# Searching expert slots in the running sums, routing earlier, and laying the routed experts between the last groups of shared experts

## The reference, cut to what matters

```python
E, K, G, TG, I, NSH, C = 32, 6, 8, 3, 176, 2, 48
logits = x @ gate_w.T                       # 4096 x 32
# 3 of 8 groups of experts are kept, softmax, then the 6 best experts of each token
topk_w, topk_idx = top_k(probs, K); topk_w = topk_w * 16
pos = cumsum(one_hot(flat_e, E))[flat_e] - 1   # place of this token in its expert's queue
valid = pos < C                             # only the first 48 tokens of an expert count
xb = buf[:E * C].reshape(E, C, h)           # gathered: 32 experts x 48 slots x 256
g, u = split(einsum('ech,ehf->ecf', xb, w_gate_up), 2)
yb = einsum('eci,eih->ech', silu(g) * u, w_down)
out = weighted sum of yb over a token's experts
gs, us = split(x @ ws_gate_up, 2)           # the shared expert, on all 4096 tokens
out = out + silu(gs) * us @ ws_down
```

## Time and profile before

| | |
|---|---|
| median of 3 runs | 2079.32 us (2078.84 to 2084.3) |
| the profiled execution | 2079.05 us, its span 2077.1 us, mean granted TensorE clock 0.866 |
| TensorE busy | 1750.2 us, 84% of the span |
| PE weight loads busy | 1091.0 us |
| VectorE, ScalarE, GpSimd busy | 1191.6, 805.7, 254.5 us |
| the mixture of experts | from about 445 to 835 us |

### The profile page before, as it was taken

One profiled execution on the slowest core, in us unless ns is written; L12 is line 12 of the kernel. 1 busy time (PEld: TensorE's weight loads), 2 busy tenths in 40 slices (PEclk: granted clock), 3 DMA queues, 4 the chain that ended last, 5 costly groups with the idle time before them and its releaser, 6 DMA issues.

```text
span 2077.1 us, 27028 instructions
## 1 busy us (share of the span) xinstructions
PE 1750.2 (84%) x10042; PEld 1091.0 (53%) x10043; DVE 1191.6 (57%) x2366; ACT 805.7 (39%) x1316; POOL 254.5 (12%) x252
## 2 busy tenths in 40 slices
PE   4999999869778996569988989987989888989897
PEld 3788888745447995323344443343533344433345
DVE  5556666451562005577755668656767666667455
ACT  4444444212230100227654227743146633157520
POOL 4334333212240000100010000000000000000000
PEclk8999999889995556758899989898988999979999
DMA  2000000040012420200000000000000000000000
GB/s 93 14 28 21 30 20 20 11 137 25 10 31 84 125 87 0 84 0 2 1 1 0 1 1 1 22 0 0 1 1 1 21 0 0 1 1 2 21 0 21
DMA packets 27139, 47.83 MB, mean 23 GB/s; under 512 B 7312, under 2 KB 16016, under 8 KB 26256
## 3 DMA queue, kind: packets, MB, share of 16 engines
q1 hardware_dynamic: 26464, 44.74, 6.6%
q0 software_dynamic: 576, 1.77, 0.3%
HBM read 37.59 MB, written 9.06 MB: 22 GB/s over the span
## 4 chain that ended last, share of the span: by engine, by line
issue 58%; POOL 2%; DVE 0%; POOLq 0%; DVEq 0%
POOL rs_sb L1251 1%; POOL ve_sb L1248 0%; POOL qks_sb L1266 0%; POOL v_sb L1265 0%; POOL qks_sb L1256 0%; DVE bn_sb L1431 0%; DVE x_sb_sb L1446 0%; POOLq L1086 0%; POOLq L65 0%; POOL qks_sb L1267 0%; DVE mv_sb L1437 0%; DVEq L1086 0%; POOL v_sb L1264 0%; DVEq L65 0%; DVEq L1435 0%
## 5 line engine op out<-in xcount | busy, mean ns | idle before, releaser
L1488 DVE TENSOR_REDUCE mx_sb<-s_ps 128x1 f32<-128x512 f32 (+1 forms) x512 | 322.7, 655 | 137.1 <-PE s_ps L1742 93.0
L1319 ACT ACTIVATE room_sb<-s_ps 128x1024 f32<-128x1024 f32 (+1 forms) x320 | 282.5, 949 | 22.7 <-PE s_ps L1766 20.0
L1739 PE MATMUL s_ps<-room_sb 48*128 48x512 f16 (+3 forms) x640 | 206.6, 355 | 18.0 <-DVE mx_sb L1483 9.6
L1766 PE MATMUL s_ps<-room_sb 51*128 51x128 f16 (+4 forms) x1152 | 155.4, 297 | 34.7 <-ACT room_sb L1319 26.5
L1786 PE MATMUL cm_ps<-room_sb,v_sb 128*32 128x512 f32 (+3 forms) x1536 | 179.3, 550 | 0.8 <-ACT room_sb L1325 0.8
L1739 PEld LDWEIGHTS s_ps<-room_sb 48*128 48x128 f16 x640 | 60.2, 99 | 225.9 <-DVE mx_sb L1488 134.3
L1248 POOL TENSOR_TENSOR ve_sb<-mv_sb,eps_sb 128x4 f32<-128x4 f32 x24 | 5.0, 210 | 1195.1 <-DVE mv_sb L1437 1195.1
L1898 PE MATMUL s_ps<-xbT_sb,w_fg_sb 128*128 128x512 f32 x256 | 132.6, 630 | 13.8 <-DVE room_sb L1534 13.0
L1911 PE MATMUL cm_ps<-w_fd_sb,room_sb 128*128 128x256 f32 x512 | 131.0, 405 | 14.2 <-DVE room_sb L1562 14.2
L1898 PE MATMUL s_ps<-xbT_sb,w_fu_sb 128*128 128x512 f32 x256 | 130.2, 620 | 0.0
L392 DVE SCALAR_TENSOR_TENSOR x_sb_sb<-xp_sb,conv_w_sb,x_sb_sb 128x512 f32<-128x512 f32 x96 | 108.5, 1139 | 22.8 <-ACT x_sb_sb L319 20.5
(11 more groups left out here) (233 smaller groups left out, 3513.3 us busy)
## 6 DMA issues: line engine op xcount, KB each, us to landing
we_gu_sb<-we_gu SPq DMA_DIRECT2D x32, 352.0 KB
we_dn_sb<-we_dn SPq DMA_DIRECT2D x32, 176.0 KB
x_in_sb<-x SPq DMA_DIRECT2D x9, 512.0 KB, 3.7
rows<-x_sb_sb SPq DMA_DIRECT2D x8, 512.0 KB, 3.0
x_sb_sb<-rows SPq DMA_DIRECT2D x2, 2048.0 KB, 12.3
out<-x_sb_sb SPq DMA_DIRECT2D x8, 512.0 KB, 2.6
xp_sb<-w_in SPq DMA_DIRECT2D x1, 1024.0 KB, 5.6
x_sb_sb<-w_up SPq DMA_DIRECT2D x1, 1024.0 KB, 6.4
```

Source lines behind the costliest of these rows:

```text
L1319: act.activation(weights[(g * NU + u) % SLOTS_P][:, 2 * pair:2 * pair + 2, 0:width(u) * P], W[s % 2][:, :, 0:width(u) * P], ACT.Exp, scale ...
L1488: dve.tensor_reduce(mx[:, pair, k % 2, slot:slot + 1], X[:, k % 2, 0:count * P], AX.X, ALU.max, negate=True).then_inc(mx_ok, 1)
L1739: last = pe.matmul(X[:, k % 2, at * P:(at + plain) * P], query[head:head + NORM, i * P:(i + 1) * P], key[head:head + NORM, j * P:(j + plai ...
L1766: last = pe.matmul(W[s % 2][:, head, (at + low - i) * P:(at + high - i) * P], key[first:first + rows, j * P:(j + 1) * P], query[first:firs ...
```

## The change

1. Slots. The 12 counting passes are replaced by two searches. `max_index` looks for eight needles (place + 1) at a time in `cum` and returns the position of the first match; eight small steps cast it, and put 4096 where the expert has too few tokens.
2. Routing ahead. The exponential comes after `gate_up(1)`, the counting matmuls after `gate_up(2)` (both were after `gate_up(4)`), the gather before GpSimd's `add(3)`.
3. From group 3 on VectorE makes the shared experts' product straight from PSUM; ScalarE's copy and GpSimd's product go away there.
4. The 24 transposes of the gathered rows lie in group 5, four behind each piece of `gate_up(5)`. `xgT` moves from `xT` into the room of `selr` and `prer` (now one tile `maps`), `yT` into the arena.
5. The 32 routed experts lie in 24 places: behind each of the four tiles of `down(5)`, `down(6)`, `down(7)`, and behind each of the six pieces of `gate_up(6)`, `gate_up(7)`. Place n takes experts 32n/24 up to 32(n+1)/24, so of each three places two have one expert and one has two (8 places with two). Expert e writes all its products into one bank, `tp[e % 2]`, and its gate matmuls wait until the output of expert e-2 is out of that bank.
6. All loops over groups and experts are written out.

```diff
+COUNT_AT = 2
+DVE_AT = 3
+GATHER_AT = 4
+SLOTS_AT = 5
+MOE_AT = 6
+MOE_SLOTS = 2 * (GT + 2 * NSX) + GT
...
+        xgT = maps[:, 0:KD * E * CAP].rearrange("p (k e c) -> p k e c", k=KD, e=E)
+        yT = view(KD, CAP, E)
...
+        def experts_at(g, i):
+            n = (g - MOE_AT) * (GT + 2 * NSX) + i
+            return range(n * E // MOE_SLOTS, (n + 1) * E // MOE_SLOTS) if g >= MOE_AT else range(0)
```

On GpSimd:

```diff
+            for g in range(1, NG):
+                if g < DVE_AT:
+                    act(g)
+                if g == GATHER_AT:
+                    gather()
+                add(g - 1)
+            add(NG - 1)
```

On ScalarE:

```diff
+            def expert_out(e):
+                wait(act, edn_mm, e + 1)
+                act.activation(yT[:, :, :, e], tp[e % 2][:, 2 * NIX * CAP:2 * NIX * CAP + KD * CAP]
+                               .rearrange("p (k c) -> p k c", k=KD), ACT.Copy).then_inc(ey_ok, 1)
+            def experts(g, i):
+                for e in experts_at(g, i):
+                    expert_gate(e)
+                    if e > 0:
+                        expert_out(e - 1)
```

On VectorE:

```diff
-            for j in range(CJ):
-                dve.wait_ge(cnt_ok, j + 1)
-                dve.tensor_scalar(dump, cum[:, :], place[:, j:j + 1], 0.0, ALU.is_le, ALU.add,
-                                  accum_out=cnt[:, j:j + 1]).then_inc(cnt_ok, 1)
+            for i in range(2):
+                last = dve.max_index(at8[i][:, :], needle[:, i * (CJ - 8):i * (CJ - 8) + 8], cum[:, :])
+            last.then_inc(cnt_ok, 1)
...
+            def shared_act(g, i):
+                wait(dve, sg_ok, NSX * g + i + 1)
+                wait(dve, gu_mm, 2 * NSX * g + 2 * i + 2)
+                if i == 0:
+                    wait(dve, dn_mm, 2 * g)
+                dve.tensor_tensor(su[:, i, :], mm[(2 * i + 1) % 4][:, :], sg[:, i, :], ALU.mult).then_inc(sa_ok, 1)
...
+            for g in range(DVE_AT, NG + 1):
+                if g == SLOTS_AT:
+                    dve.wait_ge(busy_mm, 1)
+                    dve.tensor_copy(busy[:, :], tp[0][0:1, 0:NT]).then_inc(busy_ok, 1)
+                for t in range(GT):
+                    experts(g, t)
+                if g < NG:
+                    for c in range(2 * NSX):
+                        if c % 2:
+                            shared_act(g, c // 2)
+                        if g == SLOTS_AT:
+                            for m in range(4 * c, 4 * c + 4):
+                                slot_features(m)
+                        experts(g, GT + c)
+                if g == SLOTS_AT:
+                    slot_weights()
```

On TensorE:

```diff
+            def expert_gu(e):
+                if e == 0:
+                    wait(pe, xg_ok, CJ * KD)
+                wait(pe, ring[e % RING], 32 * (e // RING + 1))
+                wait(pe, ey_ok, e - 1)
...
+            def experts(g, i):
+                for e in experts_at(g, i):
+                    expert_gu(e)
+                    if e > 0:
+                        expert_down(e - 1)
...
+            for g in range(NG + 1):
+                if g == SLOTS_AT:
+                    pe.wait_ge(cnt_ok, 1)
+                    pe.wait_ge(cum_ok, NG)
+                    pe.matmul(tp[0][0:1, 0:NT], ones_f[:, 0:1], busy_f[:, :], start=True, stop=True).then_inc(busy_mm, 1)
+                if g > 0:
+                    for t in range(GT):
+                        down(g - 1, t)
+                        experts(g, t)
+                if g == SLOTS_AT:
+                    pe.wait_ge(busy_ok, 1)
+                    pe.wait_ge(gath, 16 * CJ)
+                if g < NG:
+                    for c in range(2 * NSX):
+                        gate_up(g, c)
+                        if g == SLOTS_AT:
+                            for m in range(4 * c, 4 * c + 4):
+                                slot_features(m)
+                        experts(g, GT + c)
+                if g == COUNT_AT:
+                    counted()
+            expert_down(E - 1)
```

More of the change, by code:

```diff
@@ L731, in _, with add, gather @@
-            add(Step(None, 0, NG - 1))
+            def add(g):
+                wait(pool, so_ok, 2 * g + 2)
+                own = x_sb[:, g * GT:(g + 1) * GT, :]
+                pool.tensor_tensor(own, own, so[:, :, :], ALU.add).then_inc(r_ok, 1)
+            def gather():
+                pool.wait_ge(idx_ok, 1)
+                pool.wait_ge(w_st, 16)
+                pool.wait_ge(consts, 16 * N2)
+                for j in range(CJ):
+                    pool.indirect_dma_start(out=xg[:, j, :], out_offset=None, in_=io["rows"][:, :],
+                                            in_offset=bass.IndirectOffsetOnAxis(ap=idx[:, j:j + 1], axis=0)).then_inc(gath, 16)
@@ L733, in _ @@
+            act(0)
+            pool.wait_ge(back, 32)
+            for g in range(1, NG):
[5 more added lines that the diff above has]
+            add(NG - 1)
         @block.scalar
         def _(act):
[L735 to L756, removed]
+            def gate(g, i):
+                wait(act, gu_mm, 2 * NSX * g + 2 * i + 1)
+                if i == 0:
+                    wait(act, sa_ok, NSX * g)
+                    wait(act, dn_mm, 2 * g)
+                act.activation(sg[:, i, :], mm[(2 * i) % 4][:, :], ACT.Silu).then_inc(sg_ok, 1)
@@ L757, in _ @@
                     act.wait_ge(sub_ok, 1)
                     act.activation(ex, ex, ACT.Exp).then_inc(exp_ok, 1)
[L759 to L772, removed]
+            expert_out(E - 1)
@@ L861, in _ @@
[L861 to L867, removed]
+            dve.tensor_scalar(needle[:, :], place[:, :], 1.0, None, ALU.add)
@@ new lines, in down, with slot_features @@
+            def down(g, t):
+                if t == 0:
+                    wait(pe, sa_ok, NSX * (g + 1))
+                    wait(pe, so_ok, 2 * g)
+                for k in range(NSX):
+                    last = pe.matmul(ro[t // 2][:, t % 2, :], su[:, k, t * P:(t + 1) * P], ws_dn[:, k, :],
+                                     start=(k == 0), stop=(k == NSX - 1))
+                if t % 2:
+                    last.then_inc(dn_mm, 1)
+            def slot_features(m):
+                j, k = divmod(m, KD)
+                wait(pe, xg_ok, m - 1)
+                pe.transpose(tp[m % 2][:, 0:P], xg[:, j, k * P:(k + 1) * P], ident[:]).then_inc(tr_ok, 1)
```

211 lines of the change are left out of this document (102 added, 109 removed).

## The result

The changed kernel takes 1981.94 us (median of 4 runs, 1979.09 to 1987.84) against 2079.08 us (2075.28 to 2084.3) of the kernel before beside it: a ratio of 0.9534, 95% interval 0.9512 to 0.9556. Forecast were 1983.7 us, range 1966 to 2015. The profiled execution took 1981.23 us.

What follows compares the result with a forecast made beforehand. TensorE sets every stage's end, by work or by waiting for the routing. From 565.0 us, 115.8 us of terms end the experts at 680.8 instead of 776.2: 95.4 off 2079.05 gives 1983.7 us, range 1966 to 2015.

Steps and rivals of the forecast that it cites:

- counting: VectorE's counting for the routing, now behind gate_up(2): 6.6 us, bounds 5 and 8.
- transposes, above gate_up(5): 24 transposes spread behind the pieces of gate_up(5) add 9 us to it, bounds 6 and 12.8.
- 32 experts: Routed experts on TensorE at full clock: 2.1 us each, 67.2 us for 32.
- new wait: In eight places with two experts, the second's gate matmuls wait for ScalarE's output: about 0.6 us more each, 4.8 in all.
- uncovered chain at the end: Behind the last expert, an uncovered chain costs 1.3 us.
- falls of the clock: In the interleaved stretch, half of the eight two-expert places cost one fall each: 6 us, bounds 0 and 20.
- The clock of the experts: Shared pieces between routed experts hold TensorE's clock high: 4.33 to 2.1 us per expert, 71 us gained.
- Rival (a): Experts hold the interleaved stretch at half clock: 2079.5 us, chance 0.05; half the stretch so: 2030 us, chance 0.09.
- Rival (b): Transposes pull the clock down in group 5, six pieces at half clock adding 10.3 us: 1994 us, chance 0.08.
- Rival (c): VectorE's search runs needles one after another, 70 us instead of 8.8, and TensorE stands: 2042 us, chance 0.04.
- Rival (d): Expert weights' refills exceed 10.4 us free time, each us beyond costing 7; at 25 us each 2086 us; chance 0.02.
- gather's wait: TensorE's wait for the gathered rows ahead of the transposes, 12.2 us, goes at no price.

Runs made afterwards that it cites:

- no refills: Changed kernel with all experts behind group 7, four banks for gate matmuls, no weights loaded beyond the first four experts; 1996.36 and 2016.91 us.
- half pieces: Changed kernel with each shared gate or up piece cut into two steps, giving 36 places of at most one expert; 1969.45 us, 0.9459 of before.
- fours: Changed kernel with experts laid four at a time behind every third of the 24 places; 2028.26 us.
- the four experiments with clusters: Changed kernel with experts all at the end (2047.39 us), also with more banks (2029.88), also without refills (1996.36 and 2016.91), or four at a time (2028.26).
- pairs: Changed kernel with experts between half pieces of shared work, and group 5's transposes two behind each half piece of gate_up(5); 1966.53 us, 0.9455 of before.
- three buffers: Changed kernel with three buffers for expert weights instead of four; 1992.28 us.
- products as before: Changed kernel with shared experts' products of groups 3 to 7 left on ScalarE (copy) and GpSimd (product); 2003.37 us.
- all experts at the end with more banks: Changed kernel with all experts behind group 7, four banks for gate and up and two others for down; 2029.88 us.
- two buffers: Changed kernel with two buffers for expert weights instead of four; 2103.28 us, 1.0104 of before.

## Why the prediction was right

By its own steps, with the profiled execution after:

| step | forecast, us | measured, us |
|---|---|---|
| start of gate_up(2) | 490.2 | 493.5 |
| counting | 6.6 | 5.3 |
| gate_up(3) and pause | 11.2 | 11.3 |
| one search | 4.4 | 4.42 |
| small steps around them | 2.3 | 1.3, and 0.9 for the last cast of the counts ahead of them |
| slots there | 518.3 | 520.3 |
| gathers | 518.3 to 533.6 | 520.6 to 535.6 |
| transposes, above gate_up(5) | 9 | 8.4 |
| start of the experts' stretch | 565.0 | 566.3 |
| 12 pieces of down, 12 of gate_up | 36.5 | 16.4 + 21.4 = 37.8 |
| 32 experts | 67.2 | 32 x 2.1 = 67.2 |
| new wait, 8 times | 4.8 | 8 x 0.68 = 5.4 |
| uncovered chain at the end | 1.3 | about 0 |
| falls of the clock | 6 (four) | about 5.2 (three) |
| end of the experts | 680.8 | 682.7 |
| what follows, against before | 0 | -4.4 |

From 566.3 us the measured terms add up to 681.9; 0.8 us is left over.

**What was luck.** The experts ended 1.9 us later than forecast, and what follows them took 4.4 us less than assumed, by chance; that is why the profiled execution came out 2.5 us under the forecast and not 1.9 above it. The number of falls, half of the eight places, was a guess without a row behind it, and 2.1 us for an expert a choice between 2.03 and 2.27.

**The clock of the experts** was the one guess that could have sunk it, and its reason held: with no dense work between them the experts keep half clock even without a pause (no refills: 0.50), with dense work behind each they keep full clock (half pieces: 1.00), and the size follows the grain (fours 2028, the change 1982, halves 1969). The size, 2.1 us at full clock from the 147 ns loads at half clock, was exact to the tenth. Which property of these matmuls lets the clock fall, the 48 columns, the weight loads that set their pace or the 88 rows of the down matmuls, no run takes apart.

**Rival (a)** is what the four experiments with clusters show: it is real, and an order of the same instructions away. I gave it 0.14 and had no row for how much dense work between experts is enough; the experiments bracket it (four in a row are too many, two cost a fall in three of eight places in the profile, one costs none).

**Rival (b)** fell: with the transposes the clock was 1.00 in 548.0 to 566.3, and in pairs too. The Trainium skill (TensorE: Matmul & The Clock Gate, Part 4: PE-mode transpose) says that transposes don't count as busy work the way other matmuls do. In these traces, at 0.22 us of them for every 0.86 us of dense matmuls, they did no harm: no run here shows them as a pause.

**Rival (c)** fell by one row, 4.42 us for eight needles. **Rival (d)** stayed away, but both of its figures were too kind. The free time of a refill is not 10.4 us: in the changed kernel 7.4 to 10.0 us lie between a refill's issue and the gate matmuls that need it, mostly 8.3, since not 4 but 5 to 6 us pass before it is asked for (570.20 to 575.98 for expert 1). And a refill takes 3.7 to 5.3 us where the rows gave 3.0. With three buffers the free time goes down to 4.0 us and still no wait came; with two it happened, and cost as much again through the clock, which the rival left out.

**Mis-sized terms.** Counting was 1.3 us too long, since I scaled from half clock. The start of gate_up(2), 3.3 us late, is two falls of the clock, behind the pauses of groups 0 and 1: down(0) took 7.12 us and down(1) 7.13 us, where the kernel before had 5.44 and 5.44. They happen in some executions and not in others: the two kernels with half pieces had 1.00 from 484 to 494 us. The end chain I charged doesn't stand free, because the down matmuls of expert 30 cover it: without the fall the down matmuls of experts 30 and 31 follow each other without a gap, 1.95 us for both, in the kernel with pairs. The pieces of down and gate_up are each some 0.05 us longer between experts than in a row. And the unchanged rest took 4.4 us less (4.2 of them within the span); from the last expert to the end of the span, profiled executions have 1300.9 (before), 1296.7 (after), 1309.3 (halves), 1300.0 (pairs), 1318.3 (three buffers) and 1293.6 us (products as before), with the same instructions. The granted clock over it goes the same way: 0.90 in the shortest, 0.89, 0.88 in halves, 0.87 in the longest. So 25 us between two kernels can lie in a part that neither changed, and where two runs stand against four, the stretch itself is the better witness. Whether this is also what runs of one kernel differ by isn't shown: each kernel has one profile.

**Where the gain went and came from**, against the sum's own split: gather's wait 12.2 (11.6 come back in the kernel with products as before), experts' clock 71 (no experiment gives it alone; all experts at the end with more banks lose 48 to the change and still have some at full clock), and the search 0 by itself, about 46 as a condition of the rest.

## What to carry to other kernels

Small matmuls bound by their weight loads, as these of 48 columns, can lose TensorE's clock when they stand alone, however busy the engine is; lay each between dense matmuls in the finest grain that the banks allow, and look for the granted clock in the table of windows and not for idle time. A faster step is worth what its consumer's place in its queue lets it be worth: move the consumer first, then count. Before deepening or cutting a ring, compare the refill's own time (asked for until used) with the free time between release and use; here the edge lay between two and three buffers, with 4.0 us free at the least in the kernel with three.

## What the runs showed of the hardware

- 48-column matmuls of fp32 with TensorE busy for 10.00 of 10 us, and no gap, were granted 0.50; the clock left 1.00 without a gap, and didn't return in 100 us.
- Dense matmuls of 512 columns brought it back, but not after a fixed number: in the change within one piece (3.42 us, then 1.38 for the next gate matmuls), with four experts at a time within three (8.03 us where three take 5.4 at full clock), and with two buffers one piece of 3.75 us, with a wait of 1.1 us behind it, did not (2.58 for the next gate matmuls).
- A search of 8 needles over 4096 bf16 entries costs VectorE 4.42 us and the loading of the needles 0.07 to 0.09 us; it is the price of one counting pass (4.48 us), for eight slots instead of one.
- In a ring with two buffers, each us of waiting for weights cost about another us in clock (59.3 us of waits, 121 us more in all).
- A pair of transposes of 128 columns between dense matmuls costs TensorE 0.22 us (545.92 - 545.70) at full clock when both banks are free.
